# Four more places for raw weights in a fused cross-attention block: loads from ScalarE's queue, and the splits of the second multiplication dealt out anew

## The reference, cut to what matters

```python
x = layer_norm(hidden_states, ln1_w, ln1_b)
q, k, v = x @ q_w + q_b, ctx @ k_w + k_b, ctx @ v_w + v_b      # 16 heads of 32
out = softmax(q k^T / sqrt(32)) v
hidden = out @ cproj_w + cproj_b + hidden_states
y = layer_norm(hidden, ln2_w, ln2_b)
y = gelu(y @ fc_w + fc_b)            # 512 -> 2048, tanh form
return hidden + (y @ proj_w + proj_b) # 2048 -> 512
```

## Time and profile before

| what | us |
|---|---|
| median of 3 runs (806.45 to 811.02) | 806.96 |
| the profiled execution, its own time | 805.86 |
| its span, first to last instruction | 804.0 |
| TensorE busy | 739.1 |
| VectorE busy | 566.9 |
| GpSimd busy | 449.8 |
| ScalarE busy | 362.2 |

### The profile page before, as it was taken

One profiled execution on the slowest core, in us unless ns is written; L12 is line 12 of the kernel. 1 busy time (PEld: TensorE's weight loads), 2 busy tenths in 40 slices (PEclk: granted clock), 3 DMA queues, 4 the chain that ended last, 5 costly groups with the idle time before them and its releaser, 6 DMA issues.

```text
span 804.0 us, 10414 instructions
## 1 busy us (share of the span) xinstructions
PE 739.1 (92%) x3568; PEld 502.8 (63%) x3568; DVE 566.9 (71%) x1079; ACT 362.2 (45%) x618; POOL 449.8 (56%) x305
## 2 busy tenths in 40 slices
PE   7999999998999999999989499999785969999998
PEld 5888876633344444344357388787664848878886
DVE  6773348778888889996976378799797437763453
ACT  4434241567666656766855144422223525432221
POOL 2634040279977886897550546355376244545565
PEclk9999999999999999999999799999997979999999
DMA  8748286776845885689443512536952322222352
GB/s 314 236 145 286 86 264 186 243 196 173 210 106 157 220 213 134 173 179 224 137 81 92 183 52 80 185 103 142 225 182 74 136 78 72 86 66 93 94 193 80
DMA packets 118196, 124.24 MB, mean 155 GB/s; under 512 B 41248, under 2 KB 66084, under 8 KB 118144
## 3 DMA queue, kind: packets, MB, share of 16 engines
q1 hardware_dynamic: 118000, 123.56, 53.3%
q10 hardware_dynamic: 144, 0.02, 0.0%
HBM read 94.05 MB, written 29.37 MB: 154 GB/s over the span
## 4 chain that ended last, share of the span: by engine, by line
PE 70%; DVE 18%; issue 4%; DMA 3%; ACT 3%; SPq 2%; POOL 1%; DVEq 0%; POOLq 0%; ACTq 0%
PE ps L600 18%; PE ps L601 18%; PE ps L602 18%; DVE ps L1293 7%; PE ps L723 4%; PE ps L707 4%; PE ps L692 4%; PE ps L738 3%; DVE R L1499 2%; DMA RW<-in_fc_w 1%; DVE R L1225 1%; DVE mx L1293 1%; PE ps L660 1%; DMA yt<-FU 1%; ACT Pt L968 1%
## 5 line engine op out<-in xcount | busy, mean ns | idle before, releaser
L968 ACT ACTIVATE Pt<-ps 128x512 f32<-128x512 f32 x256 | 137.6, 597 | 71.9 <-PE ps L707 70.9
L1624 POOL TENSOR_TENSOR BIG<-RW,BIG 128x512 fp32r<-128x512 f32 x66 | 100.0, 1517 | 105.3 <-ACT BIG L1070 103.4
L1070 ACT ACTIVATE BIG<-RW 128x512 fp32r<-128x512 f32 x64 | 40.0, 631 | 133.9 <-PE ps L602 128.6
L707 PE MATMUL ps<-BIG 98*128 98x512 f32 x256 | 93.2, 440 | 3.5 <-ACT Pt L968 3.1
L1293 DVE CUSTOM_DVE_ANT_0 ps<-ps,FU 128x512 f32<-128x512 f32 x128 | 84.5, 722 | 14.9 <-PE ps L692 14.8
L1293 DVE CUSTOM_DVE_ANT_0 ps<-ps,BIG 128x512 f32<-128x512 f32 x128 | 84.6, 722 | 10.9 <-PE ps L692 10.7
L707 PEld LDWEIGHTS ps<-BIG 98*128 98x128 f32 x256 | 44.2, 187 | 67.9 <-issue 29.6
L1762 POOL TENSOR_TENSOR R<-Pt 128x1024 f32<-128x1024 f32 x20 | 47.3, 2387 | 45.9 <-ACT Pt L968 45.9
L600 PE MATMUL ps<-BIG,HR 128*128 128x512 f32 x172 | 67.4, 392 | 4.1 <-DVE HR L1411 4.1
L723 PE MATMUL ps<-Pt,V 128*32 128x512 f32 x512 | 68.2, 605 | 0.0
L602 PE MATMUL ps<-BIG,HR 128*128 128x512 f32 x172 | 67.0, 389 | 0.0
(11 more groups left out here) (174 smaller groups left out, 1732.4 us busy)
## 6 DMA issues: line engine op xcount, KB each, us to landing
RW<-in_proj_w SPq DMA_DIRECT2D x64, 256.0 KB, 2.7
BIG<-qs SPq DMA_DIRECT2D x62, 256.0 KB, 2.9
BIG<-ks SPq DMA_DIRECT2D x62, 256.0 KB, 3.1
RW<-in_fc_w SPq DMA_DIRECT2D x48, 256.0 KB, 3.1
ks<-BIG SPq DMA_DIRECT2D x32, 256.0 KB, 2.0
qs<-BIG SPq DMA_DIRECT2D x32, 256.0 KB, 5.2
R<-hd SPq DMA_DIRECT2D x20, 256.0 KB, 4.4
R<-in_x SPq DMA_DIRECT2D x16, 256.0 KB, 5.4
```

The source lines that it names most:

```text
L707: eng.matmul(bk, K_[0:98, j, kc * 128:(kc + 1) * 128], Q_[0:98, j, :], start=True, stop=True).then_inc(S["p_ra"], 1)
L968: eng.activation(Pt[:, r, j % 2, :], bank(bank_a(("s2", i, j))), ACT.Exp, scale=SCALE).then_inc(S["a_ra"], 1)
L1070: eng.activation(second(n)[0], raw_w(at), ACT.Copy).then_inc(S["a_pj"], 1)
L1624: eng.tensor_tensor(dst, src, high.bitcast(F32), ALU.subtract).then_inc(S[name], 1)
```

## The change

- **Places.** There are eight places for raw weights. Places 0 to 3 are those of RW; places 4 to 7 are V rows 12 to 15. They take only the "wr" tiles of p = 0, 1, 4 and 5. Each place has its own list, and a load waits for the use of what lay in the same place before.
- **Issue.** SyncE issues the first half's wf tiles and the wr tiles of p = 0 to 3 (the first four of these right after the wf tiles). ScalarE issues all others, 96 loads: in the first half the wr tiles of p = 4 to 7, all 64 pj tiles (tiles 0 to 3 of a half while the other products end, the rest two steps ahead of their use, one each step), and all tiles of the second half.
- **Second multiplication.** The hidden tiles' high parts move from VectorE to ScalarE (`hidden_high`), the weights' low parts from GpSimd to VectorE (`second_low`). ScalarE no longer splits weights three ahead: it does `second_high(n)`, `hidden_high(n)`, then one load, each step. The scale and shift of batches 2 and 3 move from VectorE to ScalarE (`y_scale`).
- **Order.** In the first half VectorE does the fourth wf low part and all four transposes ahead of the last division; the four cproj products come in two pairs, at p = 2 and 3; block and block_low come one p earlier, and `rest_high(0, 0)` ahead of three of the block_highs; GpSimd does the last `out_low` before all four `x_add`. At the end of the first half only one wf tile is split inside the second multiplication (before: four, on both engines, in steps 28 to 31); two more follow at the second half's start.

```diff
-        RAW_W = []
+        RAW = [[] for _ in range(8)]
         for q in range(2):
+            for k in range(4):
+                RAW[k] += [("wf", HF * q + k, 0), ("wf", HF * q + k + 4, 0)]
+                RAW[k] += [("wr", HF * q + p + k // 2, k % 2) for p in (2, 6)]
+                RAW[k] += [("pj", 2 * NF * q + n, 0) for n in range(k, 32, 4)]
+                RAW[4 + k] += [("wr", HF * q + p + k // 2, k % 2) for p in (0, 4)]
...
+        def raw_w(item):
+            k, _ = RAW_AT[item]
+            return RW.rearrange("p a (h t) -> p (a h) t", h=2)[:, k, :] if k < 4 else V[:, 8 + k, :]
...
# TensorE
-                    if q == 0 and 2 <= p < 6:
-                        if p == 2:
-                            pe.wait_ge("v_rb", NB)
-                        cproj(3, p - 2, range(4), bank(p - 2)).then_inc(S["p_cp"], 1)
+                    if q == 0 and 2 <= p < 4:
+                        pe.wait_ge("v_rb", NB)
+                        for c in (2 * p - 4, 2 * p - 3):
+                            cproj(3, c, range(4), bank(c)).then_inc(S["p_cp"], 1)
...
# ScalarE, new
+            def hidden_high(n):
+                b, f = divmod(n, NF)
+                act.wait_ge(*hidden_ready(b, f))
+                if n >= 3:
+                    act.wait_ge("p_pr", 4 * (n - 2))
...
+                eng.activation(parts_of(n)[:, 0, :], hidden(b, f), ACT.Copy).then_inc(S["a_hh"], 1)
+
+            def load_weights(item):
+                act.wait_ge(*raw_free(item))
...
+                eng.dma_start(raw_target(item), raw_source(item)).then_inc(S[raw_come(item)[0]], 16)
...
# ScalarE, end of the other products and second multiplication
-                    if p == 5:
-                        for n in range(3):
-                            second_high(32 * q + n)
+                    if 5 <= p < 7:
+                        load_weights(("pj", 32 * q + 2 * p - 10, 0))
+                        load_weights(("pj", 32 * q + 2 * p - 9, 0))
                     if p + 1 < HF:
                         gelu_rest(q, p + 1, 22)
+                    if p == 6:
+                        second_high(32 * q)
+                        hidden_high(32 * q)
+                second_high(32 * q + 1)
+                hidden_high(32 * q + 1)
+                for n in range(2, 32):
+                    m = 32 * q + n
+                    second_high(m)
+                    hidden_high(m)
+                    if n + 2 >= 4 and n + 2 < 32:
+                        load_weights(("pj", m + 2, 0))
...
# VectorE
+            def hidden_low(n):
...
+                dve.wait_ge("a_hh", n + 1)
+                eng.tensor_tensor(lo, hidden(b, f), hi.bitcast(F32), ALU.subtract).then_inc(S["v_hl"], 1)
+
+            def second_low(n):
+                dve.wait_ge("a_pj", n + 1)
+                hi, lo = second(n)
+                eng.tensor_tensor(lo, raw_w(("pj", n, 0)), hi.bitcast(F32), ALU.subtract).then_inc(S["v_pj"], 1)
...
-                    if n >= 2:
-                        split_hidden(m)
+                    second_low(m)
+                    hidden_low(m)
```

More of the change, by code:

```diff
@@ L516, in _ @@
                 if i == 52:
-                    for n in range(4):
-                        load_raw_w(n)
+                    for k in range(4):
+                        load_weights(("wf", k, 0))
                 if i == 56:
@@ new lines, in _ @@
+            load_weights(("wf", 6, 0))
+            load_weights(("wf", 7, 0))
+            for m in range(2):
+                for h in range(2):
+                    load_weights(("wr", m, h))
+            for c in range(4):
+                y_store(1, c)
+            y_load(1)
+            for h in range(2):
+                load_weights(("wr", 2, h))
+            for c in range(4):
+                if c == 2:
+                    for h in range(2):
+                        load_weights(("wr", 3, h))
+                sp.wait_ge("v_cp", c + 1)
+                eng.dma_start(hd[12 + c], R2[:, c, :]).then_inc(S[f"d_hd{c}"], 16)
@@ new lines, in _ @@
+            sp.wait_ge("g_xc", 16)
+            eng.dma_start(cbt[:, :], pj_b.partition_broadcast(128)).then_inc(S["d_pb"], 16)
+            residual(0)
+            ln2_load(2)
+            ln2_load(3)
+            for c in range(4):
+                y_store(2, c)
+            y_load(2)
+            for c in range(4):
+                y_store(3, c)
+            y_load(3)
+            store_out(0)
+            residual(1)
+            store_out(1)
+            residual(2)
+            store_out(2)
@@ L590, in _ @@
+            residual(3)
             store_out(3)
@@ L1184, in _ @@
                 for p in range(HF):
+                    if p < 4:
+                        for h in range(2):
+                            load_weights(("wr", HF * q + p + 4, h))
                     gelu_rest(q, p, 21)
@@ L1771, in _ @@
             out_low(NS - 2)
-            x_add(3, 0)
-            x_add(3, 1)
             out_low(NS - 1)
-            x_add(3, 2)
-            x_add(3, 3)
+            for c in range(4):
+                x_add(3, c)
             for q in range(2):
```

320 lines of the change are left out of this document (135 added, 185 removed).

## The result

The changed kernel takes 771.6 us in the median of 4 runs (770.9 to 773.2), the kernel before 806.8 on the same chip: a ratio of 0.9555, with a 95% interval from 0.952 to 0.959. The forecast was 774.0 in a range of 765 to 792. The profiled execution has a span of 769.7 us against 804.0, and a mean granted clock of 0.993 against 0.975.

The account below looks back on a forecast made before the run. TensorE was taken as the bound, with 52.5 us of idle time and slow clock to win from 402 us on. Terms summed to 32.9 us off the profiled 805.86, giving 773.0; with 1.1 for the runs' median, 774, range 765 to 792.

Parts of the forecast that it names:

- layer norm in the steps: First half's second multiplication, 555 to 578 us: waits for a store to yt shrink from 6.1 to 1 us, saving 5.1.
- first products, first half: 402 to 443 us: a wf low part moves ahead of transposes and division; 4.9 us becomes 2.0, saving 2.9.
- first to other products, first half: 443 to 458 us: earlier wr tiles leave a 4.0 us gap and 1.5 of slow clock from 14.4, saving 8.8.
- entries, twice: Start of the second multiplication in each half: steps 0 and 1 start late, costing 1.9 and 1.4 us.
- steps 20 to 27: 585 to 602 us: VectorE loses four y_affine; 3.9 us of waits fall to 1.0, saving 2.9.
- into the second half: 605 to 619 us: VectorE's splits no longer stand behind front_low_part; 10.9 us falls to 0.4, saving 10.5.
- first to other products, second half: 646 to 660 us: first gap grows to 3.0 with 1.5 of slow clock, second gap goes; saving 6.0 us.
- Steady steps: Second multiplication: ScalarE 1.6 and VectorE 1.38 of 2.73 us a step, 3.3 us of cover; worth nothing by itself.
- ScalarE held by its loads: Rival, slower: landing over 3.87 us or issue over 1.47 us lengthens the second multiplication's steps, 835 or 829 us; chance 0.09.
- The other products still waiting: Rival: the second wr tile stays late, waits of 9.8 and 5.35 us stay, 788 us; chance 0.21.
- the gaps are not the loads': Rival: TensorE's gaps only move behind gelu and the combining adds, nothing gained, 806 us; chance 0.07.
- VectorE crowded by GpSimd: Rival, steps 20 to 31: subtractions that meet GpSimd's work take longer, 6 us more, 780 us; chance 0.13.

Follow-up runs that it names:

- e3: The changed kernel with hidden tiles' high parts back on VectorE and weights' low parts back on GpSimd in the second multiplication: 784.2 us, ratio 0.9727.
- e5: The changed kernel with VectorE's layer-norm work of the first half dealt out over more steps: 769.6 us, ratio 0.9552.
- e6: The changed kernel with the work of ScalarE, VectorE and GpSimd around the first half's other products in another order: 769.3 us, ratio 0.9538.
- e9: The changed kernel with only the weights' low parts of the second multiplication back on GpSimd: 780.3 us, ratio 0.9662.
- e10: The changed kernel with only the hidden tiles' high parts back on VectorE: 783.4 us, ratio 0.9687.
- e12: The changed kernel with SyncE's four loads of batch 2's rows behind the stores of batch 3's second block: 769.0 us, ratio 0.9529.
- e4: The changed kernel with each pj load issued one step ahead of its use, not two, from tile 4 of a half on: 779.1 us, ratio 0.9669.
- e11: The changed kernel with the eight pj loads of the first half's steps 12 to 19 issued by SyncE between the layer-norm stores: 772.4 us, ratio 0.9559.
- e7: The changed kernel with rest_high(1, 0) and, in both halves, the second multiplication's first two pairs of high parts moved ahead of gelus: 767.3 us, ratio 0.9526.
- e1: The kernel before with the low parts of the second half's first four wf tiles taken after step 31, not in steps 28 to 31: 802.5 us, ratio 0.9947.
- e2: The kernel before with the eight places alone, all loads still issued by SyncE and all splits on the engines of before: 791.6 us, ratio 0.9828.

## Why the prediction was right

It came to 774 by its own steps, and each of them is there in the traces, but that it came so close to 771.6 is in part luck. Three terms are off by about 2 to 3 us (the layer norm in the steps by 3.0, the other products by 1.8 and 2.1), and the misses cancel. Saved, in us (the profiled executions, waits and slow matmuls):

| step | forecast | measured |
|---|---|---|
| first products, first half | 2.9 | 3.6 |
| first to other products, first half | 8.8 | 7.0 |
| entries, twice | -3.3 | -2.1 |
| layer norm in the steps | 5.1 | 2.1 |
| steps 20 to 27 | 2.9 | 3.5 |
| into the second half | 10.5 | 10.6 |
| first to other products, second half | 6.0 | 8.1 |
| sum | 32.9 | 32.8 |

The spans differ by 34.3. About 1.5 us of the measured sum is the clock's doing: the 2.35 us wait of the second half has no slow matmuls behind it here, and seven or eight in e3, e5, e6, e9, e10 and e12, where it is 2.34 to 2.44 (e4 and e11 have none).

**First products.** The wait for GpSimd's out_low before the first cproj pair was to be 1.8 us and was 1.29, with nothing ahead of it.

**Other products, first half.** The gap was to be 4.0 us and was 1.93 + 2.83, in two pieces. ScalarE's crowd showed up a step earlier than I had it, in the first products. The term for slow clock was 1.5 and was 2.6.

**Entries.** Forecast 0.7 and 1.2 us, then 0.2 and 1.2; measured 0.34 and 0.81, then 0.36 and 0.77. The links in the chain are the right ones, as e7 shows by taking them away.

**Steady steps.** VectorE's subtraction takes 0.68 us in the second half (one of 19 took 1.79), ScalarE's issue 0.33 us. The 0.69 before was not for want of GpSimd's work beside it, as I had it: GpSimd's subtraction ran beside it there too, but started second. "Worth nothing by itself" held where a step has little else in it: from 510 to 540 and from 690 to 755 us e3 loses nothing. Undone, the exchange costs 13 to 14 us. Most of it lies in the stretches of the norm and steps 20 to 31, and 3.8 us in the last steps of the second half, for which I had no term. I had not said that my terms needed both halves of it.

**Layer norm.** This is the term that is off most: 1.0 us left by the forecast, 2.65 and seven slow matmuls in the trace. The step that failed reads "VectorE still waits some 2 us for a store, inside the 3.3". It waited 6.8. I had taken the weight loads between the stores for what made this store late; with eight of them back, in e11, the buffer came free at 556.2 us in place of 557.0, so they were not what held it. SyncE's order (four norm loads ahead of the store) makes the wait, as e12 shows by taking it away, together with a landing of 6.2 us that goes with the queue's pause of 3.36 right behind.

**Into the second half.** Forecast 0.4 left, measured 0.33. By e1 the order alone, with four low parts in a row, would have brought 4 of it.

**Second half's other products.** Smaller left-over than forecast: 2.35 us and no slow clock, where 3.0 and 1.5 stood. That no slow clock came is luck, as said above.

**The rivals.** ScalarE held by its loads: its clause on issue length did not come (0.33 us at the median, 0.45 at most for these loads), and its clause on landing was built on a wrong order, as e4 showed; the decision point lies later. Seven of the 64 pj loads took more than the forecast's own limit of 3.87 us to land, up to 6.1, and all that came of it was one wait of 0.9 us. The Trainium skill's sentence that was weighed there ("Perfetto Trace Analysis", section "DMA Instruction — HWDGE (DVE, Sync)", an issue's span holds the wait for a shared generator) would have had ScalarE's issues long beside SyncE's stores: 27 of them in 505 to 590 took 334 to 352 ns, one of these at 554.47, inside the store issue that took SyncE 3.36 us. For this pair of queues the trace does not show it. The other products still waiting: e2 shows that the places alone end it in the second half and take 9.82 to 5.34 in the first, which answers the rival that the gaps are not the loads' as well. VectorE crowded by GpSimd: e9 is this rival made real, 9 us.

## What to carry to other kernels

Count TensorE's gaps with the slow matmuls behind them, stretch by stretch, and ask for each which link is second latest; terms of 2 to 10 us made this way summed to the total within 3 us, though single ones missed by up to 3 and only cancelled. When splits are dealt out over engines, look at which pairs will run together and which starts first: two subtractions on VectorE one after the other took as long here as one that starts behind GpSimd's (1.38 and 1.37 us). A queue's list deserves the same reading as an engine's: a load that waits for the last store holds back stores whose data are ready. And before a few us between two single traces are put down to an edit, look whether they are slow matmuls behind a wait that both have.

## What the runs showed of the hardware

- A DMA that stands behind two copies in ScalarE's list is issued 0.05 us after the start of the first of them, not after the end of either (rows at 537.40 above; in e12 0.13 us after the start of a y_scale). The issue costs the copies nothing that shows. Ordering one step ahead still costs some 8 us in all (e4), as landings vary.
- SyncE's queue stops once for 1.4 to 3.4 us in a series of some 30 stores of small pieces (the tile to yt, 32 x 32 blocks). It falls on a store or on a load by place: 2.38 before, 3.36 in the changed kernel, 2.00 in e11, 1.40 in e9. The store issued just ahead of it takes 2.2 to 3.2 us longer to land than the pause lasts, in all 14 traces. What in the queue it waits for, no run shows.
- When a subtraction of VectorE's and one of GpSimd's overlap, the one that starts second is the longer: VectorE's 1.37 us and GpSimd's 1.29 where GpSimd starts first (e9), 0.69 and 1.60 where VectorE does (steady steps before).
- The same idle time of TensorE costs clock in one kernel and not in the next. The 1.93 us wait of the first half, for the same copy of ScalarE's, was followed by seven or eight slow matmuls in e3, e5, e7 and e12, and by none in the changed kernel, e4, e9, e10 and e11. The wait behind it, 2.1 to 3.4 us, was the other way round: none in e3, e5, e7 and e12, 12 or 13 in the changed kernel, e4, e10 and e11. In e9 neither had any, though the second was 3.00 us:

```profile
440.24 0.58 PE L592 MATMUL ps<-YT,RY 128*128 128x512 f32 x1 [1.93 <-ACT BF L991]
...
446.94 0.47 PE L592 MATMUL ps<-SLX,BIG 128*128 128x512 f32 x1 [3.00 <-DVE BF L1417]
```

  The first row is of e7 (clock 0.55 in the 3 us from it), the second of e9 (clock 1.00). So what a wait of 1.9 to 3.0 us costs in clock, nothing or 1.4 to 2.6 us, can't be forecast from its length here.
